# Graph network kernel: in layer three VectorE adds the rows of the second slot before it copies the centred weights out of PSUM

## The chip, the cores and the metric

The kernel runs on one core of a Trainium2 chip. The metric is the device time of one execution in microseconds (us). The profile is one further execution, recorded by the hardware profiler. TensorE, VectorE, ScalarE, GpSimd and SyncE are called PE, DVE, ACT, POOL and SP in its rows.

## The reference

There are 6250 nodes with 128 features and 200,000 edges, sorted by destination. Three layers of a gated graph network (GRU) come first, then a residual and a layer norm, then three layers that count each edge once, and a residual and a layer norm again:

```python
for l in range(3):                       # gated layers
    m = x @ weight[l]
    agg = segment_sum(m[src] * edge_weight[:, None], dst, num_segments=N)
    x = gru_cell(agg, x, w_ih, w_hh, b_ih, b_hh)
x = layernorm(x0 + x)
for W, b in ((W0, b0), (W1, b1), (W2, b2)):   # counted layers
    x = relu((x + segment_sum(x[src], dst)) @ W.T + b)
x = layernorm(x1 + x)
```

## The kernel before, in words

Features lie on the 128 partitions. The nodes are 49 tiles of 128, or 14 groups of 448 columns. While the first gated layer runs, the kernel builds the dense matrix of edge weights and writes it to HBM. In the second and third gated layers the segment sum of the first 12 groups ("dense" groups, `DENSE`) is done by TensorE: `aggregate` multiplies 49 tiles of messages `Y` by 49 tiles of the matrix (98 instructions at L883). SP streams the matrix in four slabs per group through a ring in SBUF.

The last two groups (12 and 13) are not in that matrix. Their nodes are summed row by row: GpSimd's `fetch_rows` (L790 to L801) gathers 128 rows of `y_rows` in HBM by the edges' source nodes, one indirect DMA per round, 350 rounds (`ROUNDS`) per layer, into `ROW_BUFS = 10` row buffers. Round i may be issued only when VectorE has added round i - 10 (semaphore `s_acc`, L795). VectorE's `add_rows` (L1650 to L1666) waits for the round to land and then adds it, times the edge weight, into two sums: two instructions at L1662 per round, or at L1665 for the first round of a run. When all 350 rounds are added, TensorE transposes the sums (`flip_runs`, L937 to L955) and groups 12 and 13 go through the same gates as the others.

The rounds are dealt out by hand between VectorE's other duties. Slot -1 has rounds 0 to 29, each slot from 0 on has 33 more, and slot 9 has the last 23:

```python
SLOT_FIRST, SLOT_NEXT = 30, 33
def rounds_by(slot):
    return max(0, min(ROUNDS, SLOT_FIRST + SLOT_NEXT * slot))
```

One gated group takes these steps. TensorE's `gates` makes four products (12 instructions at L893 to L896), ScalarE takes two sigmoids (L1308, L1309), VectorE's `mix` makes two instructions (L1607, L1610), ScalarE takes the tanh (L1313), and VectorE's `blend` and the residual sum make four more (L1616, L1619, L1621, L1749). TensorE runs one aggregation ahead. Its order in layer three is: aggregate group 1, gates 0, aggregate 2, gates 1, aggregate 3, flip the sums of groups 0 and 1 (`flip_sums`, L1028), gates 2, aggregate 4, gates 3, and so on, with one flip per pair of groups. `gates(n)` waits for `mix(n - 1)`. After each flip VectorE works out the layer norm's `statistics` (L1731 to L1739), and ScalarE then applies the norm (`deviate`, `keep_norm`) before the sigmoids of the next group.

The centred weights belong to the layer after this one. VectorE centres and scales the rows of W0 (`scale_centred_weights`), TensorE transposes them into bank 7 of PSUM between aggregate 2 and gates 1 (L1001, L1002), and `take_centred_weights` (L1720 to L1723) copies them and a bias to SBUF:

```python
dve.wait_ge(s_bnd, 2)
sc_step(0, 10, dve.tensor_copy(wcur[:, :], ps[:, bank, 0:P]))
sc_step(0, 11, dve.tensor_copy(bcur[:, :], bg[:, 0:1]))
```

Who needs them: `flip_sums(0)` waits for the eleventh step (L1019), because it writes to bank 7, and the messages of the first counted layer (`first_messages`, L1050) read `wcur` after the last aggregation. Bank 7 and `wcur` have no other user in between.

Each engine runs its instructions in the order written, so a wait on VectorE holds all that is written behind it.

Of the kernel before, what the change touches and what calls it, by code (L numbers as in the profile page):

```python
# [94 lines left out]
def gnn_program(nc, x, src, dst, firsts, nodes, edges, edge_weight, gnn_w, w_ih, w_hh, b_ih, b_hh,  # L95
# [7 lines left out]
    with ctx:  # L103
# [1490 lines left out]
        def _(dve):  # L1594
# [8 lines left out]
            def mix(n):  # L1603
                dve.wait_ge(s_gate, FREE + n + 1)
                dve.wait_ge(s_n, START + n)
                dve.wait_ge(s_rz, START + 2 * n + 1)
                dve.scalar_tensor_tensor(out=t_t, in0=ps[:, 5, 0:GW], scalar=bhh[:, 2:3], in1=r_t,  # L1607
                                         op0=ALU.add, op1=ALU.mult).then_inc(s_gv, 1)
                dve.wait_ge(s_gv, START + GV * n + 1)
                dve.scalar_tensor_tensor(out=t_t, in0=ps[:, 4, 0:GW], scalar=bih[:, 2:3], in1=t_t,  # L1610
                                         op0=ALU.add, op1=ALU.add).then_inc(s_gv, 1)
# [35 lines left out]
            def rounds_by(slot):  # L1647
                return max(0, min(ROUNDS, SLOT_FIRST + SLOT_NEXT * slot))

            def add_rows(layer, slot):  # L1650
                for i in range(rounds_by(slot), rounds_by(slot + 1)):
                    run = min(i // RUN, RUNS - 1)
                    r = i - RUN_STARTS[run]
                    buf, done = i % ROW_BUFS, WIN * (ROUNDS * layer + i)
                    dve.wait_ge(s_row[buf], 16 * (len(range(buf, ROUNDS, ROW_BUFS)) * layer + i // ROW_BUFS + 1))
                    if r == 0 and layer:
                        dve.wait_ge(s_flipr, 2 * layer)
                    for d in range(WIN):
                        weight = run_weights[:, d, i:i + 1]
                        if r:  # L1660
                            dve.wait_ge(s_acc, done + d + 1 - WIN)
                            add = dve.scalar_tensor_tensor(out=run_sums[:, run, d, :], in0=run_rows[:, buf, :], scalar=weight,  # L1662
                                                           in1=run_sums[:, run, d, :], op0=ALU.mult, op1=ALU.add)
                        else:
                            add = dve.tensor_scalar(run_sums[:, run, d, :], run_rows[:, buf, :], weight, None, ALU.mult)  # L1665
                        add.then_inc(s_acc, 1)  # L1666
# [26 lines left out]
            def sc_step(l, k, ins):  # L1693
                ins.then_inc(s_sc, 1)
                dve.wait_ge(s_sc, sc_base(l) + k)

            def magnitudes(l):
                return dve.tensor_scalar(w_abs[:, :].bitcast(I32), wT[:, 2 * N_LAYERS + l, :].bitcast(I32), MAGNITUDE,
                                         None, ALU.bitwise_and)

            def find_scale(l, bank, k):
                sc_step(l, k, dve.tensor_reduce(x_top[:, :], x_tops[:, :], mybir.AxisListType.X, ALU.max))
                if l == 0:
                    add_rows(1, -1)
                dve.wait_ge(s_bnd, l + 1 + (l > 0))

                sc_step(l, k + 1, dve.tensor_scalar(bound[:, :], ps[:, bank, 0:1], TINY, None, ALU.max))
                sc_step(l, k + 2, dve.tensor_scalar(expo[:, :], bound[:, :].bitcast(I32), EXPONENT, None, ALU.bitwise_and))
                sc_step(l, k + 3, dve.tensor_scalar(scale[:, :], expo[:, :], -1.0, float((2 * BIAS + HALF_TOP) * ONE_EXP),
                                                    ALU.mult, ALU.add))  # L1710
                sc_step(l, k + 4, dve.tensor_scalar(unscale[:, :], expo[:, :], float(-HALF_TOP * ONE_EXP), None, ALU.add))

            def scale_centred_weights():

                sc_step(0, 7, dve.tensor_reduce(w_mean[:, :], w_raw[:, 0, :], mybir.AxisListType.X, ALU.add))
                sc_step(0, 8, dve.tensor_scalar(w_mean[:, :], w_mean[:, :], 1.0 / P, None, ALU.mult))
                sc_step(0, 9, dve.tensor_scalar(w_row[:, :], w_raw[:, 0, :], w_mean[:, 0:1], scale[:, 0:1].bitcast(F32),
                                                ALU.subtract, ALU.mult))

            def take_centred_weights(bank):  # L1720
# [4 lines that stand above are left out]
            def statistics(p, banks):  # L1725
                dve.wait_ge(s_flip0, p + 1)
                dve.wait_ge(s_norm0, START + PT * p)
                dve.sem_inc(s_mark_dve, 1)
                for bank, (k0, k1) in zip(banks, PAIR_CHUNKS):
                    for k in range(k0, k1):  # L1730
                        dve.bn_stats(halves[:, k, :], ps[:, bank, (k - k0) * P:(k - k0 + 1) * P]).then_inc(s_stat0, 1)  # L1731
                dve.wait_ge(s_stat0, STAT * p + PT)
                dve.sem_inc(s_mark_dve, 1)
                for k in range(PT):
                    dve.bn_aggr(moments[:, k, :], halves[:, k, :]).then_inc(s_stat0, 1)
                dve.wait_ge(s_std0, p + 1)
                dve.reciprocal(scales[:, bass.ds(PT * p, PT)], deviations[:, :]).then_inc(s_stat0, 1)
                dve.wait_ge(s_stat0, STAT * p + 2 * PT + 1)
                dve.scalar_tensor_tensor(out=shifts[:, :], in0=moments[:, :, 0:1].rearrange("p k o -> p (k o)"), scalar=-1.0,  # L1739
                                         in1=scales[:, bass.ds(PT * p, PT)], op0=ALU.mult, op1=ALU.mult).then_inc(s_stat0, 1)  # L1740

            def sum_group(n, g):
                mix(n)
                blend_and_sum(n, g)

            def blend_and_sum(n, g):
                blend(n, g)
                dve.wait_ge(s_gv, START + GV * (n + 1))
                dve.tensor_tensor(group(xT, g), group(xT, g), group(resT, g), ALU.add).then_inc(s_sum0, 1)  # L1749

            def first_lows(lo, hi):
                for c in range(lo, hi):
                    p, part = divmod(c, 2)
                    k0, k1 = PAIR_CHUNKS[part]
                    dve.wait_ge(s_yh, PT * p + k1)
                    for k in range(k0, k1):
                        t = PT * p + k
                        dve.scalar_tensor_tensor(out=Y_low[:, t, :], in0=ps[:, Y_BANKS[c], (k - k0) * P:(k - k0 + 1) * P],
                                                 scalar=scales[:, t:t + 1], in1=Y_high[:, t, :], op0=ALU.mult,
                                                 op1=ALU.subtract).then_inc(s_ye1, 1)  # L1760

            def last_gru_layer():
                n0 = GROUPS
                dve.wait_ge(s_kept, 16)
                sc_step(0, 1, magnitudes(0))
                find_scale(0, 6, 2)
                scale_centred_weights()
                sum_group(n0, 0)
                take_centred_weights(7)
                add_rows(1, 0)  # L1770
                sum_group(n0 + 1, 1)
                add_rows(1, 1)
                for i in range(1, DENSE // 2 - 1):
                    statistics(i - 1, (6, 7))
                    for par in range(2):
                        sum_group(n0 + 2 * i + par, 2 * i + par)
                        add_rows(1, 2 * i + par)
                statistics(DENSE // 2 - 2, (6, 7))
                sum_group(n0 + DENSE - 2, DENSE - 2)
                first_lows(0, 2)  # L1780
                sum_group(n0 + DENSE - 1, DENSE - 1)
                first_lows(2, 4)
                sum_group(n0 + GROUPS - 2, GROUPS - 2)
                first_lows(4, 6)
                sum_group(n0 + GROUPS - 1, GROUPS - 1)
                first_lows(6, 10)
                statistics(PAIRS - 2, (4, 5))
                first_lows(10, 12)
                statistics(PAIRS - 1, (6, 7))
                first_lows(12, 14)  # L1790
# [298 lines left out]
```

## Time and profile before

| | us |
|---|---|
| median of 3 runs | 3011.85 (3011.63 to 3016.44) |
| the profiled execution, time | 3010.85 |
| the profiled execution, span | 3009.1 |
| TensorE busy | 2918.5 (97%) |
| VectorE busy | 1517.5 (50%) |
| GpSimd busy | 978.8 (33%) |
| ScalarE busy | 909.4 (30%) |

The profiled execution is 1.00 us below the median, and 1.75 us of its time lie outside the span. The gated layer three lies between about 1616 and 2185 us of the span. The counted layers follow it. The rows below are from that stretch unless they say otherwise. A number in square brackets in a timeline row is how long the engine sat idle before the instruction, and what ended that.

### The profile page before, as it was taken

What the parts mean: (1) busy time and instruction counts of PE and PEld (TensorE: products, weight loads), DVE (VectorE), ACT (ScalarE), POOL (GpSimd) and SP (SyncE); (2) the same over time, 40 slices, a digit from 0 to 9 for tenths busy, and PEclk for the clock granted to TensorE, in tenths of its full rate; (3) what the DMA queues carried; (4) which work ended last, traced back from release to release, by engine and by line L of the source; (5) the groups of instructions that cost most, each with busy time, mean ns of one, the idle gap of its engine ahead of it and who ended that gap; (6) DMA issues with size and microseconds to landing.
All of it is one profiled execution on the core that took longest, in us unless ns stands there. A gap on an engine that the chain in (4) does not pass through costs nothing.

```text
span 3009.1 us, 75972 instructions
## 1 busy us (share of the span) xinstructions
PE 2918.5 (97%) x29592; PEld 1910.1 (63%) x29592; DVE 1517.5 (50%) x4498; ACT 909.4 (30%) x2123; POOL 978.8 (33%) x1219
## 2 busy tenths in 40 slices
PE   5999999999999999999999999999799999999998
PEld 4888888888888875555555554444455555555554
DVE  5788888888888823555551355555520010001111
ACT  5666666666666620000002001101220010001111
POOL 3222222222232325777770477777300000000000
PEclk9999999999999999999999999999899999999999
DMA  5556555556555679889895888887458868786884
GB/s 184 219 246 247 245 241 231 232 238 248 245 245 226 242 295 386 317 317 344 319 355 200 345 310 298 310 302 292 157 228 304 305 254 305 306 305 251 309 309 161
DMA packets 150159, 817.85 MB, mean 272 GB/s; under 512 B 19204, under 2 KB 28744, under 8 KB 135208
## 3 DMA queue, kind: packets, MB, share of 16 engines
q1 hardware_dynamic: 121256, 755.56, 64.3%
q0 software_dynamic: 27216, 54.53, 5.7%
q10 hardware_dynamic: 1584, 6.43, 0.5%
q8 instruction: 59, 0.97, 0.1%
q14 instruction: 44, 0.36, 0.0%
HBM read 567.58 MB, written 248.86 MB: 271 GB/s over the span
## 4 chain that ended last, share of the span: by engine, by line
PE 83%; DMA 7%; DVE 3%; POOL 3%; issue 2%; ACT 1%; ACTq 0%; SPq 0%; POOLq 0%; DVEq 0%
PE ps L1082 26%; PE ps L1161 20%; PE ps L883 18%; PE ps L1154 12%; DMA ring<-y_rows,ring 6%; POOL ring L798 3%; DVE ring L1662 2%; PE ps L893 1%; PE ps L894 1%; PE ps L1174 1%; DMA ring<-adj_w 1%; PE ps L1175 1%; PE ps L1061 1%; PE ps L896 0%; PE ps L895 0%
## 5 line engine op out<-in xcount | busy, mean ns | idle before, releaser
L883 PE MATMUL ps<-ring,Y 128*128 128x448 f32 x2352 | 890.5, 540 | 0.9 <-DMA ring<-adj_w 0.9
L798 POOL DMA_INDIRECT ring<-y_rows,ring x700 | 674.6, 964 | 394.8 <-DVE ring L1662 158.9
L1082 PE MATMUL ps<-ring,Y 128*128 128x448 f16 x4116 | 780.6, 352 | 0.0
L1538 ACT ACTIVATE ring<-ps 128x392 f16<-128x392 f32 (+1 forms) x1568 | 655.1, 506 | 289.7 <-PE ps L1154 280.5
L883 PEld LDWEIGHTS ps<-ring,Y 128*128 128x128 f32 x2352 | 447.4, 190 | 438.4 <-issue 435.7
L1082 PEld LDWEIGHTS ps<-ring,Y 128*128 128x128 f16 x4116 | 402.8, 98 | 373.8
L1161 PE MATMUL ps<-ring,Y 128*128 (+1 forms) x2744 | 616.0, 367 | 0.4 <-ACT shared L1500 0.4
L1662 DVE SCALAR_TENSOR_TENSOR ring<-ring 128x128 f32<-128x128 f32 x1384 | 402.5, 347 | 364.0 <-DMA ring<-y_rows,ring 360.1
L1161 PEld LDWEIGHTS ps<-ring,Y 128*128 128x128 f32 x2744 | 492.2, 190 | 15.6 <-ACT shared L1500 0.8
L1154 PEld LDWEIGHTS ps<-shared 64*128 64x128 bf16 x18816 | 333.8, 94 | 119.5 <-ACT ring L1538 86.5
L1938 DVE TENSOR_TENSOR shared<-shared 128x400 bf16<-128x400 bf16 x1176 | 396.0, 391 | 0.0
L1154 PE MATMUL ps<-shared 64*128 64x49 bf16 (+1 forms) x18816 | 377.6, 190 | 14.7 <-issue 12.2
L1934 DVE TENSOR_TENSOR shared<-iota_lo,shared 128x1024 bf16<-128x1024 bf16 x392 | 278.9, 711 | 0.0
L1832 DVE TENSOR_REDUCE x_tops<-xT x28 | 17.4, 620 | 482.3 <-ACT xT L1448 482.3
L1448 ACT ACTIVATE xT<-ps,bcur,unscale 128x448 f32 (+1 forms) x42 | 30.4, 725 | 681.5 <-PE ps L1082 681.5
L1932 DVE TENSOR_TENSOR shared<-iota_key,shared 128x400 bf16<-128x400 bf16 x392 | 148.1, 378 | 118.5 <-PE ps L1154 105.1
L682 POOL DMA_INDIRECT shared<-in_edges,take_now x60 | 60.4, 1007 | 361.2 <-PE ps L1154 357.8
L1292 ACT ACTIVATE shared<-ps 128x448 f32<-128x448 f32 x24 | 13.0, 543 | 512.7 <-PE ps L883 512.7
L1798 DVE TENSOR_TENSOR shared<-shared,ps 128x384 f32 (+3 forms) x14 | 8.7, 621 | 227.9 <-PE ps L1097 227.6
L645 POOL COPY shared<-shared 112x128 f32<-112x128 f32 x29 | 13.9, 478 | 183.8 <-DVE shared L1891 183.8
L1313 ACT ACTIVATE shared<-shared 128x448 f32<-128x448 f32 x28 | 16.1, 576 | 182.6 <-DVE shared L1610 182.6
L893 PE MATMUL ps<-shared,wT 128*128 128x448 f32 x112 | 54.5, 569 | 15.1 <-DVE shared L1610 15.1
(177 smaller groups left out, 1376.0 us busy)
## 6 DMA issues: line engine op xcount, KB each, us to landing
ring<-adj_w SPq DMA_DIRECT2D x72, 2688.0 KB
adj_w<-ring SPq DMA_DIRECT2D x56, 2744.0 KB, 12.3
ring<-adj_h SPq DMA_DIRECT2D x42, 2800.0 KB, 9.4
ring<-adj_h SPq DMA_DIRECT2D x42, 2688.0 KB, 9.2
adj_h<-ring SPq DMA_DIRECT2D x56, 1372.0 KB, 5.0
ring<-adj_w SPq DMA_DIRECT2D x24, 2912.0 KB
ring<-y_rows,ring POOLq DMA_INDIRECT x700
y_rows<-Y ACTq DMA_DIRECT2D x2, 3136.0 KB, 15.1
```

The source lines that it names most:

```text
L682: pool.indirect_dma_start(out=edges_now[:, par, d * SHARE:d * SHARE + OWN, :].bitcast(I32) .rearrange("p e k -> p (e k)"), out_offset=None ...
L798: pool.indirect_dma_start(out=run_rows[:, i % ROW_BUFS, :], out_offset=None, in_=y_rows, in_offset=bass.IndirectOffsetOnAxis(ap=run_edges[ ...
L883: mm = pe.matmul(ps[:, bank, 0:GW], Y[:, h, :], ring[:, s, :, h - h0, :], start=(h == 0), stop=(last and h == TILES - 1))
L893: pe.matmul(ps[:, bank, 0:GW], wT[:, c, :], aggS[par], start=True, stop=False)
L1082: mm = pe.matmul(ps[:, par, 0:GW], part[:, h, :], ring_h[:, par, s, :, h - h0, :], start=(h == 0 and part is Y_high), stop=(h == TILES - 1 ...
L1154: mm = pe.matmul(sums, hot_lo[slots, buf, w, :], rhs, start=(part == 0), stop=(part == WPARTS - 1))
L1161: mm = pe.matmul(ps[:, AGG_BANK, 0:SPAN], Y[:, h, :], strip_w[:, bass.ds(slot, 1), :, h, :].rearrange("p o b c -> p (o b) c"), start=(h == ...
L1538: act.activation(strip[:, :, c0:c0 + UNIT * WIN].rearrange("p h (d j) -> p d h j", d=WIN), psum_unit(a)[:, :, kind, :, :].rearrange("p d j ...
L1662: add = dve.scalar_tensor_tensor(out=run_sums[:, run, d, :], in0=run_rows[:, buf, :], scalar=weight, in1=run_sums[:, run, d, :], op0=ALU.m ...
L1932: dve.tensor_tensor(in_pairs(hot[:, buf, :, 0, :]), every_window(iota_key, WIDE), values(par, 0, k, WIDE), ALU.is_equal).then_inc(s_hot, 1)
L1934: dve.tensor_tensor(in_pairs(hot_lo[:, buf, :, :]), every_window(iota_lo, P), values(par, 1, k, P), ALU.is_equal).then_inc(s_hot, 1)
L1938: dve.tensor_tensor(in_pairs(hot[:, buf, :, 1 + part, :]), in_pairs(hot[:, buf, :, 0, :]), values(par, 2 + part, k, WIDE), ALU.mult).then_ ...
```

## The change

In `last_gru_layer` of VectorE two calls change places. The rows of slot 0 of layer three (the second slot, rounds 30 to 62) are added before the centred weights are copied. Nothing is added or taken away, and no other engine's program changes.

```diff
                 find_scale(0, 6, 2)
                 scale_centred_weights()
                 sum_group(n0, 0)
+                add_rows(1, 0)
                 take_centred_weights(7)
-                add_rows(1, 0)
                 sum_group(n0 + 1, 1)
                 add_rows(1, 1)
                 for i in range(1, DENSE // 2 - 1):
```

## Rows read from the trace of the kernel before

**Rows 1.** The page: the chain that ended last, by engine and by line.
```profile
PE 83%; DMA 7%; DVE 3%; POOL 3%; issue 2%; ACT 1%; ACTq 0%; SPq 0%; POOLq 0%; DVEq 0%
PE ps L1082 26%; PE ps L1161 20%; PE ps L883 18%; PE ps L1154 12%; DMA ring<-y_rows,ring 6%; POOL ring L798 3%; DVE ring L1662 2%; PE ps L893 1%; PE ps L894 1%; PE ps L1174 1%; DMA ring<-adj_w 1%; PE ps L1175 1%; PE ps L1061 1%; PE ps L896 0%; PE ps L895 0%
```

**Rows 2.** Timeline of DVE in layer three (start us, us, what, count).
```profile
1701.32 0.63 DVE L1749 TENSOR_TENSOR xT<-xT,shared 128x448 f32<-128x448 f32 x1
1733.47 0.29 DVE L1722 COPY late<-ps 128x128 f32<-128x128 f32 x1 [31.53 <-PE ps L1002]
...
1733.98 4.82 DVE L1662 SCALAR_TENSOR_TENSOR ring<-ring 128x128 f32<-128x128 f32 x18
...
1768.16 0.68 DVE L1607 SCALAR_TENSOR_TENSOR shared<-ps,bhh,shared 128x448 f32<-128x448 f32 x1
...
1772.72 2.18 DVE L1662 SCALAR_TENSOR_TENSOR ring<-ring 128x128 f32<-128x128 f32 x8
...
1810.10 1.48 DVE L1731 BATCH_NORM_STATS2 averager<-ps 128x6 f32<-128x128 f32 x7
...
1822.55 2.18 DVE L1662 SCALAR_TENSOR_TENSOR ring<-ring 128x128 f32<-128x128 f32 x8
...
2086.96 3.23 DVE L1662 SCALAR_TENSOR_TENSOR ring<-ring 128x128 f32<-128x128 f32 x12
...
2150.09 1.48 DVE L1731 BATCH_NORM_STATS2 averager<-ps 128x6 f32<-128x128 f32 x7
```

**Rows 3.** Timeline of POOL: first and last gather, and each pause over 0.35 us.
```profile
1652.93 0.94 POOL L798 DMA_INDIRECT ring<-y_rows,ring  x1 [77.93 <-DMA y_rows<-Y]
...
1702.41 0.94 POOL L798 DMA_INDIRECT ring<-y_rows,ring  x1 [0.30 <-issue]
1734.87 1.07 POOL L798 DMA_INDIRECT ring<-y_rows,ring  x1 [31.52 <-DVE ring L1662]
...
1823.43 1.07 POOL L798 DMA_INDIRECT ring<-y_rows,ring  x1 [5.17 <-DVE ring L1662]
...
1911.29 1.07 POOL L798 DMA_INDIRECT ring<-y_rows,ring  x1 [4.43 <-DVE ring L1662]
...
2000.39 1.07 POOL L798 DMA_INDIRECT ring<-y_rows,ring  x1 [5.84 <-DVE ring L1662]
...
2087.84 1.07 POOL L798 DMA_INDIRECT ring<-y_rows,ring  x1 [3.93 <-DVE ring L1662]
...
2144.84 0.94 POOL L798 DMA_INDIRECT ring<-y_rows,ring  x1 [0.30 <-issue]
```

**Rows 4.** The chain of work, one piece: a gather from issue's end to landing.
```profile
1761.63 5.45 DMA ring<-y_rows,ring
```

**Rows 5.** Timeline of PE in layer three.
```profile
1733.16 0.27 PE L1002 MATMUL ps<-ident,late 128*128 128x128 f32 x1
...
1737.78 36.99 PE L883 MATMUL ps<-ring,Y 128*128 128x448 f32 x98
1774.61 0.93 PE L1028 MATMUL ps<-ident,xT 128*128 128x128 f32 x7
...
1819.54 0.99 PE L893 MATMUL ps<-shared,wT 128*128 128x448 f32 x2 [2.65 <-DVE shared L1610]
...
2126.15 1.76 PE L1028 MATMUL ps<-ident,xT 128*128 128x128 f32 x7 [7.95 <-DVE xT L1749]
...
2156.23 1.19 PE L947 MATMUL ps<-ident,ring 128*128 128x32 f32 x4 [11.87 <-ACT shared L1292]
```

**Rows 6.** Waits of PE, 1616 to 2200 us (total us, times, longest).
```profile
PE ps L893 <- DVE shared L1610: 14.5, 6, 4.2
```

**Rows 7.** Timeline of ACT: the first sigmoid of group 1.
```profile
1737.98 0.63 ACT L1308 ACTIVATE shared<-ps,brz 128x448 f32<-128x448 f32 x1 [4.08 <-PE ps L896]
```

**Rows 8.** Busy time by stretch (us, each engine busy, PE clock, DMA share, GB/s).
```profile
core 0: us, PE busy (x) PEld busy (x) DVE busy (x) ACT busy (x) POOL busy (x), PEclk, DMA share, GB/s
...
2156.00:2163.00 7.00, 6.77 (x31) 6.71 (x32) 3.96 (x7) 4.80 (x11) 0.00 (x0) 0.52 0.01 2
```

## The prediction

> **What bounds the kernel now.** I read the page's chain first. TensorE holds 83% of it, so most of the program runs at TensorE's pace. But 6% of the span is "DMA ring<-y_rows" (the landing of gathered rows), 3% POOL L798 (issuing them) and 2% DVE L1662 (adding them) [rows 1]. Together that is some 11%, or 330 us, in which a loop of gather, land and add sets the end. I then looked for the stretch where this happens, and found it in layer three, from 1733 us to 2150 us. TensorE's timeline of that stretch shows the sign. TensorE waits for others, first at 1819.54 (2.65 us), then up to 7.95 us at 2126.15 and 11.87 us at 2156.23 [rows 5]. Its short waits for `mix` come to 14.5 us in six [rows 6]. With the two long ones that makes 34.3 us. So layer three is not bound by TensorE. It ends when the 350th round has been added, for `flip_runs` of group 13 must wait for it.
>
> The second view is GpSimd's timeline, which sets the pace of that loop. Rounds 0 to 39 are issued from 1652.93 to 1702.41, 39 steps in 49.48 us, or 1.27 us each. Then GpSimd pauses for 31.52 us, the longest pause of the layer [rows 3]. From round 40 at 1734.87 to round 349 at 2144.84 are 309 steps in 409.97 us. Four more pauses come to 5.17 + 4.43 + 5.84 + 3.93 = 19.37 us, and the rest is 390.6 / 309 = 1.26 us a step [rows 3]. So, between pauses, GpSimd issues without rest, and VectorE's 0.54 us per round (18 adds in 4.82 us [rows 2]) is not the limit.
>
> The third view says whose fault the long pause is. VectorE ends the residual sum of group 0 at 1701.32 + 0.63 = 1701.95 and does nothing until 1733.47, when it copies the centred weights: idle 31.53 us, released by PE L1002 [rows 2]. That transpose runs at 1733.16, behind a whole aggregation [rows 5]. Behind the waiting copy stand the adds of slot 0. The ten row buffers fill, round 40 has no buffer, and GpSimd stands still.
>
> **What the change does, part by part.** The two small copies (0.29 us and a one-column copy) stay, so no work is removed. The 66 adds of slot 0 start at 1701.95 instead of 1733.98. What each then meets:
>
> Issue. Round 39 leaves at 1702.41 and is done at 1703.35. Round 40 needs round 30 added. Its first add starts at 1701.95, and in the trace the first new gather follows the first add by 1734.87 - 1733.98 = 0.89 us, so it would be free at 1702.84. GpSimd reaches it after its usual 0.30 us, at 1703.65. Round 40 thus moves from 1734.87 to 1703.65, by **31.2 us** [rows 2, 3]. That is the main term.
>
> End of slot 0. Its last round is 62, 22 steps of 1.26 us behind round 40: issued at 1731.4, busy 0.94 us, landed 5.45 us later [rows 3, 4], so at 1737.8, and added at about 1738.3. In the trace, the slot ended at 1768.16 [rows 2]; 31.2 us off that is 1737.0. I take 1737.0 to 1738.3. Then the weights are copied, 0.5 us (1733.98 - 1733.47 [rows 2]), with no wait, since the transpose was done at 1733.4. This costs nothing on the path, because the next step, `mix(1)`, cannot start before the sigmoid at 1737.98 + 0.63 = 1738.6 [rows 7]. Against a rigid shift of 31.2 us VectorE is thus up to 1.7 us late here. `sum_group(1)` takes 1772.72 - 1768.16 = 4.6 us [rows 2], so slot 1 starts by about 1743.3 or 1743.5. Does GpSimd pause for that? Round 72 is the last that it may issue before round 63 is added. By its pace round 73 is due at 1703.65 + 33 x 1.26 = 1745.2, and round 63 is added by 1744.1. So it does not pause, with 1 us to spare. If it did, the cost would be under 2 us.
>
> Slot 1 and the first statistics. Round 95 ends slot 1 at 1810.10 - 31.2 = 1778.9. The statistics need TensorE's flip, which ends at 1774.61 + 0.93 = 1775.5 [rows 2, 5]. There are 3.4 us of margin. From there the pause of VectorE for statistics, norm, sigmoid, mix and blend is 1822.55 - 1810.10 = 12.4 us as before [rows 2]. It contains two engines' work in a fixed order, so GpSimd pauses its 4 to 6 us again at each of the four pairs [rows 3].
>
> Does TensorE become the limit further on? A pair of groups costs TensorE two aggregations of 36.83 us, two gates of 4.5 us and one flip of 0.77 us, 83.5 us (the aggregation at 1737.78 and the flip at 1774.61 start 36.83 apart [rows 5]). VectorE and GpSimd take (2086.96 - 1822.55) / 3 = 88.1 us a pair [rows 2]. So TensorE gains 4.6 us per pair on them, and the first margin of 3.4 us is the tightest. Free of waits, TensorE does the fourth flip at 1774.61 + 3 x 83.5 = 2025.1, then gates 8, aggregation 10, gates 9 and three quarters of aggregation 11 until 2099.6. After a flip, the last slab (12 of 49 tiles, 9.0 us), gates 10 and the eight transposes of group 12 (about 1 us) it is ready at about 2115. `flip_runs` of group 13 starts, by my shift, at 2156.23 - 31.2 = 2125.0. TensorE still waits about 9 us there. The gain is therefore not cut off by TensorE, and from there on all follows in the same order, to the end.
>
> The sum: -31.2 us, against the profiled execution 3010.85 - 31.2 = 2979.65 us. The median of the runs shown is 1.00 us higher, so 2980.7 us.
>
> Small terms. The flips behind the last wait ran at a granted clock of 0.52 [rows 8], which is 1.2 GHz for nearly all of it. With a wait of 9 us in place of 11.87 us I expect the same, term 0. If the clock were full there, about half of 6.5 us, some 3 us, would be gained too. The moved gathers run beside the stream of the matrix. So do all others, and the pace of 1.26 us already holds with it. Term 0, with one late landing as bound. A landing takes 5.45 us of a loop of ten buffers, 12.6 us, and is hidden unless it is the last of a slot. I allow 4 us either way.
>
> One rule bears on this. Gathers that were issued while VectorE was idle took 0.94 us (round 0), and those beside the adds 0.94 to 1.07 us [rows 3]. The Trainium skill, "SBUF — State Buffer", section "Who interferes with whom", says that a VectorE instruction with two SBUF inputs blocks a GpSimd instruction that reads SBUF, and the other way round, for its full length. By that rule the moved adds would hold up each gather of the slot, and the time would be that of rival 1's first case, 2987; by the rows, which show at most 0.13 us of it, it is 2980.7.
>
> **The rivals.**
> 1. GpSimd and VectorE hinder each other in the moved slot. If each of the 23 gathers of rounds 40 to 62 waited for one add of 0.27 us (4.82 / 18 [rows 2]) more than now, the gain would be 31.2 - 6.2 = 25 us, about 2987. Against it: rounds issued beside adds show no such thing. With it go the other ways to give part back: a late landing at a slot's end, or a statistics step that now waits for its flip (over 3.4 us late). They would give 2984 to 3004. Chance 0.14.
> 2. More than forecast. GpSimd's four later pauses (19.4 us) shrink because the phases fall differently. Then TensorE is the limit at 2115 us, the gain is 41 us, 2971. For it: a margin of 9 us. Against it: the pause comes from the 12.4 us of statistics, which do not move. Chance 0.06.
> 3. The gain is lost altogether, with no change to tell. This needs another work behind round 349 that ends late anyway. The candidate is TensorE, which by the sum above is ready at 2115. Chance 0.03.
> 4. Slower. The weights' copy now stands behind 33 rounds, and `flip_sums(0)` waits for it (L1019). It decides from the point at which slot 0 ends after 1774.6, 72.7 us after its start, against some 36 us as I count. From there TensorE's chain is put off one for one, and it has 9 us until it is the limit and 31.2 us more until the gain is eaten, so the total is worse once slot 0 takes over 72.7 + 40 = 113 us. That is a step of 3.4 us over its 33 rounds in place of 1.26; at 3.7 us a step (123 us) the time would be about 10 us above before, 3021. Chance 0.03.
>
> **How the numbers follow.** The forecast itself (27 to 36 us gained, 2976 to 2985) has 0.74. Measurements of this kernel tell about 0.2% (6 us) from no change. Faster by more than that: 0.74 + 0.14 + 0.06 less a little of rival 1, 0.93. Within: 0.04. Slower: 0.03. The range reaches down to rival 2 at its edge, 2971, and up to 2990, which takes in rival 1's main case, and leaves out about 0.1 to 0.15.
>
> **What the profile after would show.** DVE L1722 has no 31.5 us before it and starts at 1737 to 1739; the adds begin at 1702. GpSimd has no pause over 2 us before the first statistics, and four of 4 to 6 us after. The last gather is issued near 2113.6 and the statistics that were at 2150.09 start near 2119. TensorE's waits for `mix` at L893 (14.5 us) and the 7.95 us at the flip are gone, and 9 us remain before L947. If instead the wait before L947 is near 0, rival 2 holds. If GpSimd's step between pauses grows past 1.26 us, rival 1 does. A wait at L1028 for DVE L1723 would be rival 4. The prediction is wrong if VectorE's 31.5 us come back anywhere between 1702 and 2119.

## The result, and the profile after

The changed kernel took 2977.92 us in the median of 4 runs (2976.41 to 2980.32), the kernel before 3013.16 us in the median of 4 (3011.63 to 3016.44). The ratio is 0.9882, with a 95% interval of 0.9865 to 0.9899. That is 35.2 us faster, and 30 to 41 us by the interval. The forecast was 2980.7 us, a gain of 31.2 us. The profiled execution of the changed kernel took 2976.41 us (span 2974.7), 34.4 us less than that of before.

The timeline of DVE after the change answers to [rows 2]:

```profile
1699.48 0.63 DVE L1749 TENSOR_TENSOR xT<-xT,shared 128x448 f32<-128x448 f32 x1
1700.03 6.38 DVE L1662 SCALAR_TENSOR_TENSOR ring<-ring 128x128 f32<-128x128 f32 x24
...
1734.35 0.28 DVE L1722 COPY late<-ps 128x128 f32<-128x128 f32 x1
...
1736.91 0.68 DVE L1607 SCALAR_TENSOR_TENSOR shared<-ps,bhh,shared 128x448 f32<-128x448 f32 x1 [2.10 <-ACT shared L1308]
...
1776.14 1.47 DVE L1731 BATCH_NORM_STATS2 averager<-ps 128x6 f32<-128x128 f32 x7
...
2115.35 1.48 DVE L1731 BATCH_NORM_STATS2 averager<-ps 128x6 f32<-128x128 f32 x7
```

The adds start where VectorE stood idle. The copy has no wait ahead of it, since the transpose was done before the slot ended. The next step, L1607, waits 2.10 us for ScalarE's sigmoid, so the copy cost nothing there, as the prediction had it.

The timeline of POOL after, with the same choice of rows as [rows 3]; the third row is round 40:

```profile
1651.45 0.94 POOL L798 DMA_INDIRECT ring<-y_rows,ring  x1 [76.66 <-DMA y_rows<-Y]
...
1700.57 0.94 POOL L798 DMA_INDIRECT ring<-y_rows,ring  x1 [0.30 <-DVE ring L1662]
1701.82 0.95 POOL L798 DMA_INDIRECT ring<-y_rows,ring  x1 [0.30 <-DVE ring L1662]
...
1789.46 1.07 POOL L798 DMA_INDIRECT ring<-y_rows,ring  x1 [3.95 <-DVE ring L1662]
...
1878.90 1.07 POOL L798 DMA_INDIRECT ring<-y_rows,ring  x1 [5.75 <-DVE ring L1662]
...
1965.50 1.08 POOL L798 DMA_INDIRECT ring<-y_rows,ring  x1 [3.18 <-DVE ring L1662]
...
2051.46 1.07 POOL L798 DMA_INDIRECT ring<-y_rows,ring  x1 [2.96 <-DVE ring L1662]
...
2108.89 0.99 POOL L798 DMA_INDIRECT ring<-y_rows,ring  x1 [0.30 <-DVE ring L1662]
```

The pause of 31.52 us is gone. Four short ones are left, 15.84 us in all, where before had 19.37.

TensorE's timeline after, and its waits from 1616 to 2180 us, against [rows 5, 6]:

```profile
1731.33 0.27 PE L1002 MATMUL ps<-ident,late 128*128 128x128 f32 x1
...
1735.95 36.99 PE L883 MATMUL ps<-ring,Y 128*128 128x448 f32 x98
1772.78 0.93 PE L1028 MATMUL ps<-ident,xT 128*128 128x128 f32 x7
...
2097.56 0.93 PE L1028 MATMUL ps<-ident,xT 128*128 128x128 f32 x7
...
2121.49 1.19 PE L947 MATMUL ps<-ident,ring 128*128 128x32 f32 x4 [8.61 <-ACT shared L1292]
```

```profile
PE ps L947 <- ACT shared L1292: 8.6, 1, 8.6
PE ps L893 <- DVE shared L1610: 1.6, 2, 0.8
```

TensorE now runs without a stop from 1731 us to the row sums of group 13, and waits 8.61 us there. The 1.6 us for `mix` lie behind those row sums, as two waits of the same length do in the kernel before. So TensorE is not yet the limit of the layer, but 8.6 us from it.

Where the 34.4 us of the profiled pair lie, going along the chain:

| piece | before | after | less by |
|---|---|---|---|
| start of the layer's gathers | 1652.93 | 1651.45 | 1.5 |
| first gather to round 40 | 81.94 | 50.37 | 31.6 |
| round 40 to the last gather | 409.97 | 407.07 | 2.9 |
| last gather to the row sums of group 13 | 11.39 | 12.60 | -1.2 |
| row sums to the end of the span | 852.87 | 853.21 | -0.3 |

The 31.6 us are the change, forecast 31.2. The 2.9 us are the shorter pauses (3.5 us) less a pace of 1.266 in place of 1.264 us. The first line lies ahead of the changed instructions, so it is scatter.

Seen from TensorE, the stretch from the first gather to the row sums fell from 503.3 us with 470.5 us busy to 470.0 us with 461.4 us busy. Some 24 us of the gain are thus waits that went away, and some 9 us are work that took longer behind those waits, at a lower granted clock: 0.97 over the stretch before, 0.99 after.

### The profile page after: what moved, and what is told of

Read it like the earlier page. It is cut to its first block, busy times and chain, and to the rows that moved or that the text cites. A ratio compares the mean times of both kernels' runs of the same rounds, so it can differ in the third digit from the quotient of the medians.

```text
span 2974.7 us, 75973 instructions
## 1 busy us (share of the span) xinstructions
PE 2908.7 (98%) x29592; PEld 1906.0 (64%) x29592; DVE 1514.6 (51%) x4498; ACT 910.1 (31%) x2123; POOL 980.6 (33%) x1219
## 4 chain that ended last, share of the span: by engine, by line
PE 84%; DMA 7%; DVE 4%; issue 2%; POOL 1%; ACT 1%; ACTq 0%; SPq 0%; DVEq 0%; POOLq 0%
PE ps L1082 26%; PE ps L1161 20%; PE ps L883 18%; PE ps L1154 12%; DMA ring<-y_rows,ring 6%; DVE ring L1662 2%; POOL ring L798 1%; PE ps L893 1%; PE ps L894 1%; PE ps L1174 1%; DMA ring<-adj_w 1%; PE ps L1175 1%; PE ps L1061 1%; PE ps L896 0%; PE ps L895 0%
## 5 line engine op out<-in xcount | busy, mean ns | idle before, releaser
L1662 DVE SCALAR_TENSOR_TENSOR ring<-ring 128x128 f32<-128x128 f32 x1384 | 400.8, 347 | 366.2 <-DMA ring<-y_rows,ring 363.2
L676 POOL TENSOR_SCALAR take_now<-steps_in,leap_start 112x2 int32<-112x2 f32 x30 | 29.1, 971 | 122.6 <-DVE late L1867 122.6
L1607 DVE SCALAR_TENSOR_TENSOR shared<-ps,bhh,shared 128x448 f32<-128x448 f32 x28 | 19.1, 682 | 88.0 <-ACT shared L1308 87.9
```

## The experiments

They ran on chips 1, 2, 3 and 13 by their numbers. The number of the chip of the first pair, which I call the first chip, is not on record; whether the chip or its condition at that time makes the difference described here is not known. On the four chips the kernel before took 3343 to 3362 us in the median, 330 to 348 us more than in the first pair. In the groups of the second and third gated layers TensorE and VectorE went through a stretch in which they started one instruction per 1.3 to 2.8 us. I call it the crawl. It is in every profile taken on these chips, in the layers whose rows are gathered by indirect DMAs, and it shifts what limits the layer. So the first runs answer the questions only in part, and later ones were made to remove it. In experiment kernels the helper's new lines move line numbers: L1665 there is L1662, L1725 is L1722.

**The change again**, 5 rounds on chip 1 and 5 on chip 2.

> The changed kernel once more, beside the kernel before, to narrow the ratio. By the theory (GpSimd's gathers start again 31.2 us earlier, and the four later pauses are shorter by a few us) the gain is 31 to 35 us, ratio 0.9885 to 0.9897. By the rival that part of the first 35.2 us was scatter between runs, it falls below 31 us, ratio over 0.9897.

> The changed kernel again. In the four runs before this one the chip ran the kernel before in 3347 us, not 3013, and TensorE and VectorE started one instruction per 1.3 to 2.8 us for some 20 us in each group of the gated layers. If this chip shows no such stretches, the theory wants 31 to 35 us gained, ratio 0.9884 to 0.9897. If it shows them, some 15 us, ratio 0.995 to 0.997.

Chip 1: 3332.12 us against 3347.25, ratio 0.9959 (0.9945 to 0.9973). Chip 2: 3347.84 against 3361.59, 0.9964 (0.9951 to 0.9976). So the change is worth 12 to 15 us there. The first expectation failed. Its rival had the ratio (over 0.9897), but not the reason: it was no scatter but the crawl. The second expectation, written with the crawl in sight, came in. In TensorE's timeline of the first of these runs (chip 1), the crawl looks like this:

```profile
1867.70 0.54 PE L883 MATMUL ps<-ring,Y 128*128 128x448 f32 x1 [2.24 <-issue]
1870.50 0.91 PE L883 MATMUL ps<-ring,Y 128*128 128x448 f32 x1 [2.27 <-issue]
1873.30 0.91 PE L883 MATMUL ps<-ring,Y 128*128 128x448 f32 x1 [1.89 <-issue]
```

"Issue" says that TensorE waited for nothing the profile shows. The same run in stretches of 5 us (stretch, us, busy of each engine, PE clock, DMA share, GB/s):

```profile
1855.00:1860.00 5.00, 5.00 (x14) 2.47 (x13) 2.39 (x8) 0.00 (x0) 3.78 (x5) 1.00 1.02 396
1860.00:1865.00 5.00, 5.00 (x15) 2.47 (x13) 3.10 (x11) 0.00 (x0) 3.78 (x5) 1.00 0.53 189
1865.00:1870.00 5.00, 1.00 (x3) 0.37 (x2) 1.88 (x7) 0.00 (x0) 3.78 (x5) 1.00 0.21 52
1870.00:1875.00 5.00, 1.81 (x2) 0.58 (x2) 1.30 (x4) 0.00 (x0) 3.78 (x5) 0.52 0.20 52
...
1890.00:1895.00 5.00, 2.99 (x7) 0.98 (x6) 0.00 (x0) 0.00 (x0) 1.89 (x2) 0.94 0.34 63
1895.00:1900.00 5.00, 5.00 (x15) 2.53 (x14) 0.00 (x0) 0.00 (x0) 0.00 (x0) 1.00 0.98 404
...
1935.00:1940.00 5.00, 5.00 (x15) 2.58 (x14) 3.48 (x13) 0.00 (x0) 3.78 (x5) 1.00 0.21 52
1940.00:1945.00 5.00, 2.02 (x5) 0.76 (x5) 1.78 (x6) 0.00 (x0) 3.78 (x5) 1.00 0.20 52
```

As long as the stream of the matrix moves (about 400 GB/s), TensorE is full beside five gathers per 5 us. When the stream pauses and only the gathers are left (52 GB/s), it falls to 2 or 3 instructions in 5 us and to a clock of 0.5, in most groups after some 6 us of such a pause, as at 1935 us. It recovers when the gathers stop. On the first chip the changed kernel's pauses of the stream last 5 to 6 us, too short to compare. But the kernel before has one of 14 us there, from 1912 us, with the same queues and without the crawl:

```profile
1917.00:1922.00 5.00, 5.00 (x15) 2.54 (x14) 2.42 (x9) 0.00 (x0) 3.78 (x5) 1.00 0.21 52
1921.00:1926.00 5.00, 5.00 (x15) 2.57 (x14) 2.55 (x9) 0.00 (x0) 3.78 (x5) 1.00 0.21 50
```

**Eleven of 33 rounds ahead of the copy.**

```diff
-                add_rows(1, 0)
+                add_rounds(1, rounds_by(0), rounds_by(0) + 11)
                 take_centred_weights(7)
+                add_rounds(1, rounds_by(0) + 11, rounds_by(1))
```

> Only the first 11 of the 33 rounds of the slot stand before the copy, the other 22 behind it. Theory (GpSimd's pace sets the layer): each round moved lets GpSimd issue one gather more before it stops, so the gain is 11 x 1.26 = 13.9 us of the full one, about 2999 against 3013 before, and GpSimd's pause near 1733 is 31.5 - 13.9 = 17.6 us. Rival A (VectorE's own work is what was late): the gain is the work moved, 11 x 0.54 = 6 us, 3007. Rival B (the gain hangs on the wait as a whole, all or nothing): about 3013.

> As for the first run of this kernel: theory 11 x 1.26 = 13.9 us gained against the kernel before, and a pause of GpSimd of 17.6 us near 1733. Rival A (VectorE's own work) 6 us. Rival B (the wait as a whole, all or nothing) 0.

Chip 1: 3336.53 us, ratio 0.9976 (0.9962 to 0.9989), or 8 us gained (4 to 13). Chip 2: 3355.22, 0.9982 (0.9968 to 0.9996), or 6 us (1 to 11). Neither interval holds the theory's 13.9 us. Both hold rival A's 6 us, and both hold a third of what the whole change gives there (12 to 15 us), which is what a gain in step with the rounds moved would be. All or nothing (rival B) is out. GpSimd's pause behind the 11 rounds, the second of these rows, comes near the theory's 17.6 us:

```profile
1910.65 1.08 POOL L798 DMA_INDIRECT ring<-y_rows,ring  x1 [18.08 <-DVE ring L1665]
...
1942.78 1.08 POOL L798 DMA_INDIRECT ring<-y_rows,ring  x1 [18.35 <-DVE ring L1665]
```

That proves little. The first row is a pause of the same length where no copy waits, and the same trace has one of 14 to 20 us at each later slot. So neither the pause nor the time shows what a round moved is worth, and the run is inconclusive between a gain in step with the rounds and rival A.

**The copy one slot later still**, behind slot 1 and just ahead of the statistics.

```diff
                 add_rows(1, 0)
-                take_centred_weights(7)
                 sum_group(n0 + 1, 1)
                 add_rows(1, 1)
+                take_centred_weights(7)
```

> The copy of the centred weights stands behind the rows of the third slot too, just ahead of the first statistics. Here it is later than TensorE's flip wants it (VectorE ends the slot near 1776, the flip was at 1772.8). Theory: TensorE waits some 4 us at the flip, VectorE then waits some 1.5 us for the flip, and only that 1.5 us reaches the end, since TensorE has 8.6 us in hand before the last row sums: 1 to 3 us slower than the changed kernel, 2979 to 2981, and the last wait before L947 falls to about 6 us. Rival (each us by which TensorE is late counts): 4 us or more slower, over 2982.

3335.37 us, ratio 0.9963 (0.9950 to 0.9976), beside 0.9959 for the changed kernel on the same chip. The medians differ by 3.2 us and the ratios by 1.3 us, inside both intervals, so theory and rival can't be told apart. The wait at the flip that both sides forecast was not there to be tested. TensorE crawled and came to the flip last, so its rows have no wait for VectorE, and VectorE waited 9.60 us for it:

```profile
2024.67 1.49 DVE L1734 BATCH_NORM_STATS2 averager<-ps 128x6 f32<-128x128 f32 x7 [9.60 <-PE ps L1028]
```

It shows that the copy can stand a whole slot later at little cost on these chips, no more.

**Four rounds behind the statistics**, in each of the four pairs of the loop, where VectorE would wait 4.9 us for ScalarE.

```diff
                     statistics(i - 1, (6, 7))
+                    early = rounds_by(2 * i) + 4
+                    add_rounds(1, rounds_by(2 * i), early)
                     for par in range(2):
                         sum_group(n0 + 2 * i + par, 2 * i + par)
-                        add_rows(1, 2 * i + par)
+                        add_rounds(1, rounds_by(2 * i + par) if par else early, rounds_by(2 * i + par + 1))
```

> The changed kernel, and in each of the four pairs the first four rounds of the even slot are added right behind the statistics, while ScalarE still works, and not behind the group's sum. Theory: GpSimd's four pauses (15.8 us together) vanish, the last round is added 10 us or more earlier, and TensorE becomes the limit: the 8.6 us before L947 go to 0 to 1, time 7 to 9 us below the changed kernel, about 2970. Rival A (VectorE in a fixed order is the limit, and the four rounds push the mix back): GpSimd's pauses go, but mix starts 1 us or more later each pair and the total stays within 3 us of the changed kernel. Rival B (the landing of the rows is the limit): the pauses move and the last round ends where it did.

> As for the first run of this kernel: theory, GpSimd's four later pauses vanish and TensorE becomes the limit at the last row sums, 7 to 9 us below the changed kernel, the wait before L947 0 to 1 us. Rival A (mix is pushed back): within 3 us of the changed kernel. Rival B (landing is the limit): the same as the changed kernel, with the pauses moved.

Chip 1: 3309.94 us, ratio 0.9887 (0.9871 to 0.9902). Chip 2: 3327.44, 0.9903 (0.9882 to 0.9923). That is 22 and 20 us below the changed kernel on the same chips (3332.12 and 3347.84), and the intervals lie apart. It beats both kernels there, by more than the theory gave, and the expected step, from a wait of 8.6 us before L947 to none, can't be its reason: with the crawl, the changed kernel had no such wait. GpSimd's pauses did not vanish on these chips either. Those at the statistics, of some 20 us in the changed kernel, are cut in two, as here on chip 1. The others, of some 15 us, stay:

```profile
2025.97 1.07 POOL L798 DMA_INDIRECT ring<-y_rows,ring  x1 [9.75 <-DVE ring L1665]
...
2035.36 1.07 POOL L798 DMA_INDIRECT ring<-y_rows,ring  x1 [4.57 <-DVE ring L1665]
```

From the first gather to the row sums this kernel takes 619 us with 505.85 us of TensorE busy, and the changed one 641 us with 511.95 us. So 16 of the 22 us are time in which TensorE started nothing, most of it crawl, and 6 us are busy time at the lower clock. What the edit is worth without the crawl was not run.

**The last statistics after 12 of the 23 rounds of the last slot**, on top of that.

```diff
-                        add_rounds(1, rounds_by(2 * i + par) if par else early, rounds_by(2 * i + par + 1))
+                        last = 2 * i + par == DENSE - 3
+                        add_rounds(1, rounds_by(2 * i + par) if par else early,
+                                   rounds_by(2 * i + par) + 12 if last else rounds_by(2 * i + par + 1))
                 statistics(DENSE // 2 - 2, (6, 7))
+                add_rounds(1, rounds_by(DENSE - 3) + 12, ROUNDS)
                 sum_group(n0 + DENSE - 2, DENSE - 2)
```

> As fill4, and the last statistics stand after 12 of the 23 rounds of the last slot. Theory: with the pauses filled TensorE is the limit, so the second edit adds nothing: within 2 us of fill4. Rival (the last round and the 6.1 us from it over statistics, norm and evacuation to the row sums still set the end): 4 to 6 us below fill4.

3324.58 us, ratio 0.9892 (0.9873 to 0.9911), 2.9 us below the kernel without the split on the same chip, with intervals that overlap widely. It lies between the two forecasts, and the run can't tell them apart.

**The kernel before, profiled on chip 3.**

> The kernel before once more, for its profile on the chip of these runs. Theory: the change takes away only as much as TensorE has to wait for the row sums; on this chip TensorE crawls beside the gathers and is itself close to the limit, so here the trace shows a wait of 12 to 15 us before L947 (as much as the change gained in the timed runs), and GpSimd pauses over 31 us between rounds 39 and 40. Rival (the crawl itself changes): no wait before L947, but a longer crawl, that is more idle time of TensorE put down to issue, than in the changed kernel.

3346.51 us, one run. The theory's wait before L947 is not there: the row sums follow on the products of gates without a pause.

```profile
2493.68 0.92 PE L896 MATMUL ps<-xT,wT 128*128 128x448 f32 x2
2494.43 1.50 PE L947 MATMUL ps<-ident,ring 128*128 128x128 f32 x12
```

GpSimd's pause is longer than on the first chip, and what comes after it differs:

```profile
1942.46 1.07 POOL L798 DMA_INDIRECT ring<-y_rows,ring  x1 [49.95 <-DVE ring L1662]
```

```profile
1893.00:1942.00 49.00, 49.00 (x132) 24.72 (x132) 6.13 (x17) 2.83 (x5) 0.00 (x0) 0.99 0.83 329
1942.00:2049.00 107.00, 69.62 (x152) 31.25 (x151) 49.70 (x162) 9.44 (x17) 63.87 (x66) 0.74 0.49 172
2049.00:2164.00 115.00, 90.45 (x222) 43.95 (x221) 47.36 (x159) 9.98 (x18) 63.89 (x66) 0.85 0.63 229
```

While the gathers stand still, TensorE is busy for 49.00 of 49 us. In the next 107 us, with 66 gathers, it is idle for 37.4 us, where the next pair of groups, with as many gathers, has 24.6 us. From first gather to row sums the kernel before takes 656 us (idle 140.7), the changed one 641 us (idle 129.1, on chip 1). So the theory's wait is out, and the rival fits: what the change saves on these chips is crawl, not a wait for rows. That rests on one trace of each kernel, from two chips.

**Plain DMAs of rows in layer three, in both orders** (chip 3). The sums of groups 12 and 13 are then of other rows.

```diff
+                    if layer:
+                        pool.dma_start(run_rows[:, i % ROW_BUFS, :],
+                                       y_rows[P * (i % TILES):P * (i % TILES + 1), :])\
+                            .then_inc(s_row[i % ROW_BUFS], 16)
+                        continue
                     pool.indirect_dma_start(out=run_rows[:, i % ROW_BUFS, :], ...
```

> The changed kernel, but in layer three GpSimd reads 128 rows in a row of y_rows with a plain DMA, not the rows of the edges' sources with an indirect one, so the sums of the last two groups are of other rows. Same bytes, same waits. Theory A of the crawl (it belongs to the indirect gathers): TensorE's idle time put down to issue falls in layer three from some 20 us a group to a few, and the time drops by 150 us or more. Theory B (any transfer of GpSimd's queue beside an idle stream does it): no drop.

> The kernel before with the same plain DMAs in layer three. If the crawl is gone and the pace of GpSimd's issues is still near 1.26 us, this pair repeats the change as on the first chip: theory 31 to 35 us more than plain_after. If the pace is 0.8 us or less, the rows are no longer the limit, TensorE is, and the change is worth 0 to 10 us. If the crawl stays, 12 to 15 us as before.

Changed order 3151.15 us (3150.77 to 3152.09), order of before 3150.76 us (3149.27 to 3158.11), both against 3343.67 for the kernel before: ratios 0.9422 (0.9396 to 0.9447) and 0.9425 (0.9397 to 0.9454). Two things follow. The crawl belongs to the indirect gathers (theory A): with the same bytes and buffers the time is 192 us less. One execution shows both: in the changed order TensorE loses 98 us to "issue" in layer two, where the gathers are still indirect, and none in layer three. Not separated is whether it is the indirect form or the scattered source rows (the plain DMAs read 128 rows in a row). The quicker pace is the third candidate, and the next run answers it. And at GpSimd's new pace of 0.54 us an issue the change is worth nothing, 0.4 us the other way. The pause is still there in the order of before, and longer, but TensorE is busy for 460 of 460 us:

```profile
1919.90 0.54 POOL L799 DMA_DIRECT2D ring<-y_rows  x1 [55.75 <-DVE ring L1666]
```

```profile
1838.00:2298.00 460.00, 460.00 (x1253) 234.30 (x1252) 249.70 (x849) 51.02 (x92) 186.59 (x350) 1.00 0.87 327
```

So an idle VectorE and a standing GpSimd cost nothing by themselves. They cost when the gathers' pace leaves no time to catch up.

**The order of before with plain DMAs, slowed down** (chip 13): two small GpSimd instructions behind each DMA.

```diff
+                        for k in range(2):
+                            pool.wait_ge(s_index, INDEX_STEPS * (GATHERS + 3) + 2 * i + k)
+                            pool.tensor_scalar(leap_f[:, :], n_leaps[:, :], -1.0, float(LAST_LEAP), ALU.add, ALU.min)\
+                                .then_inc(s_index, 1)
```

> The kernel before with the plain DMAs in layer three (rows of other nodes, so the sums of the last two groups are of other rows), and two small GpSimd instructions behind each, whose result nobody reads, to bring the pace from 0.54 to some 1.2 us a round without indirect gathers. Theory: with that pace the rows set the end again and GpSimd's pause behind round 39 costs its full length: TensorE waits for mix, at the flip and before the row sums of group 13 as in the trace of before on the first chip, at 1.26 us a round some 43 us in all (34.4 us to the changed kernel and 8.6 + 0.8 left there) over plain_before, 3194 us; each 0.01 us off that pace moves it by 3 us (310 rounds). Rival (the pause costs little by itself, the first chip's 34 us came from something else): within 10 us of plain_before.

3186.28 us (3183.45 to 3187.69), ratio 0.9525 (0.9501 to 0.9550) to a kernel before of 3342.58. That is 35.5 us above the same order at full pace on chip 3, or 33 us by the ratios, each taken on its own chip. The pause and the waits of [rows 3, 5] are back, without a crawl:

```profile
1919.26 0.58 POOL L799 DMA_DIRECT2D ring<-y_rows  x1 [34.20 <-DVE ring L1670]
```

```profile
2003.09 0.99 PE L901 MATMUL ps<-shared,wT 128*128 128x448 f32 x2 [1.84 <-DVE shared L1618]
...
2263.59 0.99 PE L901 MATMUL ps<-shared,wT 128*128 128x448 f32 x2 [3.15 <-DVE shared L1618]
...
2303.64 1.75 PE L1036 MATMUL ps<-ident,xT 128*128 128x128 f32 x7 [7.49 <-DVE xT L1757]
...
2332.93 1.19 PE L955 MATMUL ps<-ident,ring 128*128 128x32 f32 x4 [11.10 <-ACT shared L1300]
```

Plain DMAs alone in flight at this pace, for longer than the crawl took to set in, leave TensorE full:

```profile
2307.00:2312.00 5.00, 5.00 (x11) 2.36 (x11) 3.79 (x14) 0.00 (x0) 4.55 (x13) 0.76 0.20 63
2312.00:2317.00 5.00, 5.00 (x14) 2.47 (x13) 2.46 (x8) 0.00 (x0) 4.47 (x14) 1.00 0.18 54
```

The rival (within 10 us) is out. The theory's size was 43 us at 1.26 us a round, less 3 us for each 0.01 us of pace. The pace between pauses came out at 1.19 us, which by that rule gives some 21 us, well short of what was measured. The rule was wrong, because a quicker pace fills the ten buffers sooner and the pauses get longer. From round 40 to the last it was 2320.63 - 1919.26 = 401.4 us, against 409.97 before, 8.6 us less, and 43 - 8.6 = 34.4 us fits the measured 35.5. That fit was made after the result.

The changed order was not run at this pace, so the run does not show by itself how much of the 35.5 us is the pause and how much the slower pace. An estimate from the traces puts it on the pause: in the changed kernel on the first chip TensorE was only 8.6 us short of being the limit at 1.266 us a round, and 1.19 us a round would take 309 x 0.07 = 22 us off that loop. TensorE, and not the pace, would then set the end of the changed order.

## Why the prediction was right, point by point

**What bounds the layer.** Confirmed where it was measured: with the pause gone, TensorE's waits for `mix` fell from 14.5 to 1.6 us, and the 7.95 us at the flip vanished. The plain and the slowed run point the same way: the order of before takes as long as the changed one at 0.54 us a round, and some 35 us longer at 1.19.

**The main term, 31.2 us.** Round 40 moved by 33.05 us, 1.48 us of which had gone before the layer's gathers began: 31.6 us.

**The end of slot 0.** Forecast 35.0 to 36.3 us behind the slot's start, measured 1734.35 - 1700.1 = 34.3 us. The copy cost nothing, and GpSimd did not pause behind it: its first pause is that at the statistics.

**The first statistics.** Forecast 3.4 us of margin behind the flip, measured 1776.14 - 1773.71 = 2.4 us. It was the tightest place, and it held.

**TensorE as the next limit.** Forecast ready at 2115 and waiting 9 us, though the prediction's own numbers (2125.0 less 2115) make it 10. It was ready at 2112.9, with all of the layer 1.8 us earlier, and waited 8.61 us.

**The pauses at the statistics.** Forecast unchanged, measured 3.5 us shorter together. This is the one term that was off, and the larger part of the difference between 31.2 and 34.4 us. The rest is the earlier start of the layer, against a slower way from the last gather to the row sums. The 35.2 us of the medians hold a further bit of chance: the kernel before has one more run in them than the prediction knew, and its median is 1.3 us higher. None of these is large beside the interval of the ratio.

**The clock behind the last wait.** No change was forecast there, and the stretch after it, counterpart of [rows 8], bears it out: granted clock 0.50, which is 1.2 GHz, where before had 0.52.

```profile
2121.00:2128.00 7.00, 6.51 (x30) 6.54 (x31) 3.78 (x6) 4.84 (x10) 0.00 (x0) 0.50 0.01 2
```

**Rival 1, GpSimd held up by the adds.** At the start of the moved slot VectorE is busy for 5.00 of 5 us, and five gathers take 3.78 us, as many as beside a half idle VectorE:

```profile
1700.00:1705.00 5.00, 5.00 (x14) 2.47 (x13) 5.00 (x20) 0.00 (x0) 3.78 (x5) 1.00 0.21 56
```

From round 40 to 62 the gathers took 28.00 us, 22 steps of 1.27 us (1729.82 - 1701.82), as many as before beside the same adds (1762.88 - 1734.87 = 28.01). It did not happen.

**Rival 2, 41 us.** Its mechanism was seen in small part: the pauses shrank by 3.5 us, not by 19, and the gain was not cut off by TensorE. **Rival 4**, the late copy, stayed 38 us from its point.

What the prediction did not see is that the gain depends on where the kernel runs. On those of the experiments it is 12 to 15 us, for TensorE there has no wait for rows with or without the change. The forecast is right for a chip without the crawl, and no row of the kernel before on the first chip shows the crawl. Shown is that the crawl goes when plain DMAs of consecutive rows stand in for the indirect gathers, and that it comes when only the gathers are in flight. That the change saves crawl time is read from two traces on different chips, one each. Why these chips crawl and the first did not, and what TensorE waits for in it, stays open. On the first chip, the step from 11 rounds to 33 was not measured.

## What to carry to other kernels

Ask of a wait on an in-order engine what stands behind it, and whether that feeds a ring: here a copy that nobody needed for 40 us held up adds, the adds held up ten buffers, and they held up the slowest pace in the layer. Put such a wait behind the work that frees buffers, up to the point where its own reader comes. Then check the price against the pace: an idle stretch of 31.5 us was worth some 31 us where the ring's issuer had no time in hand, and nothing where it could catch up at 0.54 us a round. And measure such a gain where the kernel will run: on two other chips it was less than half.

## What the hardware showed that was not expected

Indirect gathers of 128 rows of 512 bytes, one per 1.25 us, with no other transfer in flight, went with one TensorE instruction per 2.1 to 2.8 us and two adds of VectorE per 2.8 us in the traces of chips 1, 2 and 3. Plain DMAs of the same size did not, on chips 3 and 13, nor did the indirect gathers on the first chip in 14 us. GpSimd needs 0.54 us for such a plain DMA, back to back, and 0.94 us for the indirect one. VectorE's adds beside it did not lengthen the indirect one (0.94 to 0.95 us each from 1700 us of the changed kernel). The same program took 3013 us in the first pair and 3343 to 3362 us on four chips, and one edit was worth 35 us in the one and 12 to 15 us on two of the others.
